# TensorE's tile loop takes in its first turn, and GpSimd holds the scatter of list two until that turn's matmuls are issued

## The reference: what is computed

```python
logits = jnp.einsum('btd,ed->bte', x, Wr)
probs = jax.nn.softmax(logits / TEMPERATURE, axis=-1)
topk_vals, topk_idx = jax.lax.top_k(probs, TOPK)            # TOPK = 2, E = 8
router_weights = topk_vals / topk_vals.sum(-1, keepdims=True)
gate = jnp.einsum('btk,btke->bte', router_weights, one_hot)
h = jax.nn.silu(jnp.einsum('btd,efd->btef', x, W1))         # DFF = 512
y = jnp.einsum('btef,edf->bted', h, W2)
out = jnp.einsum('bte,bted->btd', gate, y)
```

## Time and profile before

| | us |
|---|---|
| three runs, median (lowest, highest) | 1382.2 (1380.06, 1385.12) |
| the profiled execution | 1379.32 |
| its span, first to last instruction | 1377.4 |
| PE busy in the span | 962.4 (70%) |
| DVE busy | 857.2 (62%) |
| ACT busy | 729.5 (53%) |
| POOL busy | 445.7 (32%) |
| the chain that ended last: PE 38%, DVE 22%, "issue" 21%, ACT 13% | |
| mean granted clock of TensorE, as a share of 2.4 GHz | 0.858 |

### The profile page before, as it was taken

The page is one execution under the profiler, slowest core; times in us unless marked ns, Lnnn a source line. Parts: engine busy times, 40 slices in busy tenths (PEclk is TensorE's granted clock), DMA queues, the critical chain, the costliest instruction groups (busy, mean ns, idle before and its releaser), DMA issues.

```text
span 1377.4 us, 30644 instructions
## 1 busy us (share of the span) xinstructions
PE 962.4 (70%) x10082; PEld 815.0 (59%) x10083; DVE 857.2 (62%) x2598; ACT 729.5 (53%) x1364; POOL 445.7 (32%) x535
## 2 busy tenths in 40 slices
PE   4888888884999999999997402111698977676740
PEld 2777777773888888888886301000587866555530
DVE  3688888885788888888885730000454666566552
ACT  3666766653776767767763300000575765555531
POOL 3123333332010010010102357777002055654555
PEclk8989998887999999999997555555799999899985
DMA  6930000000001000000000002111233334443431
GB/s 193 290 87 15 15 15 15 15 9 18 13 11 21 10 11 17 10 19 10 0 1 1 1 38 71 51 59 52 55 93 86 92 95 106 99 107 99 101 87 53
DMA packets 157233, 73.72 MB, mean 54 GB/s; under 512 B 76034, under 2 KB 151042, under 8 KB 157188
## 3 DMA queue, kind: packets, MB, share of 16 engines
q1 hardware_dynamic: 148996, 56.34, 15.6%
q0 software_dynamic: 8192, 16.79, 4.2%
HBM read 22.76 MB, written 37.75 MB: 44 GB/s over the span
## 4 chain that ended last, share of the span: by engine, by line
PE 38%; DVE 22%; issue 21%; ACT 13%; another core or an unknown queue 2%; POOL 2%; DMA 1%; DVEq 1%; ACTq 0%; SPq 0%; POOLq 0%
PE bank L449 9%; PE bank L451 8%; PE bank L450 8%; PE bank L551 4%; DVE at L925 4%; DVE X L1002 3%; ACT XTa L746 3%; DVE mx L909 3%; ACT qzh L746 3%; PE bank L537 3%; PE bank L528 2%; DVE st L992 2%; ACT vz_self L755 1%; DVE z L937 1%
## 5 line engine op out<-in xcount | busy, mean ns | idle before, releaser
L424 POOL DMA_INDIRECT wst<-yd,pos x128 | 129.9, 1015 | 222.2 <-DVE z L1117 105.6
L449 PE MATMUL bank<-XTa,qzh 128*128 128x128 f16 x768 | 146.0, 226 | 37.7 <-ACT XTa L746 37.7
L925 DVE TENSOR_TENSOR at<-bank,rc 64x32 f32<-64x32 f32 (+1 forms) x768 | 153.5, 200 | 14.4
L831 ACT ACTIVATE pr<-bank 128x512 f32<-128x512 f32 x96 | 57.3, 597 | 192.4 <-remote 106.5
L760 ACT ACTIVATE pr<-bank 128x512 f32<-128x512 f32 x192 | 114.1, 594 | 79.5 <-PE bank L528 78.3
L909 DVE TENSOR_REDUCE mx<-bank 128x8 bf16<-128x512 f32 x192 | 132.9, 692 | 28.7 <-PE bank L451 23.1
L451 PE MATMUL bank<-XTa,qzl 128*128 128x128 f16 x768 | 146.5, 226 | 0.0
L450 PE MATMUL bank<-XTa,qzh 128*128 128x128 f16 x768 | 146.3, 226 | 0.0
L764 ACT ACTIVATE pt<-bank 128x512 f32<-128x512 f32 x192 | 113.3, 590 | 60.5 <-PE bank L537 60.1
L411 POOL DMA_INDIRECT xd<-XTa,pos x128 | 123.8, 968 | 65.3 <-issue 65.3
L1098 DVE TENSOR_TENSOR xtl<-xs,xth 128x512 f16<-128x512 f32 x96 | 66.4, 695 | 120.4 <-ACT xth L832 71.5
(11 more groups left out here) (202 smaller groups left out, 3084.5 us busy)
## 6 DMA issues: line engine op xcount, KB each, us to landing
yd<-at SPq DMA_DIRECT2D x96, 128.0 KB
xd<-blank SPq DMA_DIRECT2D x2, 3072.0 KB, 20.7
X<-x_dram SPq DMA_DIRECT2D x16, 256.0 KB, 2.8
wst<-w_dram SPq DMA_DIRECT2D x16, 256.0 KB, 2.7
xd<-blank SPq DMA_DIRECT2D x1, 4096.0 KB, 28.3
cin<-ctx_in_dram SPq DMA_DIRECT2D x16, 256.0 KB, 2.8
out_dram<-z SPq DMA_DIRECT2D x16, 256.0 KB
xd<-blank SPq DMA_DIRECT2D x1, 2048.0 KB, 21.5
```

The source lines that it names most:

```text
L424: nc.gpsimd.indirect_dma_start(out=yg[k][:, t, :], out_offset=None, in_=yd[chunk_of(n)], in_offset=bass.IndirectOffsetOnAxis(ap=pos[k][:, ...
L449: nc.tensor.matmul(out_, lh, rh, start=start, stop=False, **kw)
L831: nc.scalar.activation(s32[n % 4][:], bank[n % 4][:], ACT.Silu, scale=IWS)
L925: m = nc.vector.tensor_tensor(dst, src, r, ALU.mult)
```

## The change

Three edits. The straight copy of turn 0 goes, and the loop begins at turn 0; the word with the experts is moved into the loop's register ahead of it. Since the loop's first turns now also wait on `f_ev` (`down` waited from tile 2 on only), GpSimd adds 2 to `f_ev` beforehand by a memset of one column, and all waits on it are raised by 2. And GpSimd, before it scatters list two, waits until `f_h` is 10: the `up` matmuls of tiles 0 to 4, which stand 12 matmuls ahead of turn 0's end.

```diff
--- before.py
+++ after.py
@@ -272,7 +272,7 @@
                 sp.dma_start_transpose(xt[k], xd_v[c][bass.ds(n, 1)].rearrange("o r c -> (o r) c")).then_inc(ld_t[k], 16)
 
             def store(c, n, k):
-                wait_apart(sp, f_ev, n + CB[c] + 1, ld_w, 96)
+                wait_apart(sp, f_ev, n + CB[c] + 3, ld_w, 96)
                 sp.dma_start(yd_v[c][bass.ds(n, 1)].rearrange("o p r d -> p (o r) d"), yb[k]).then_inc(y_free[k], 16)
 
             def put(g):
@@ -387,6 +387,7 @@
             pool.wait_ge(sems["self"]["fin"], G)
             attention(CROSS, G)
             pool.wait_ge(sems["cross"]["fin"], G)
+            nc.gpsimd.memset(z2[:, 1, 0:1], 0.0).then_inc(f_ev, 2)
             nc.gpsimd.memset(z[:, 0, 0:1], 0.0).then_inc(z_free, 16)
             nc.gpsimd.memset(z2[:, 0, 0:1], 0.0).then_inc(f_fin, 1)
             for k in range(4):
@@ -404,6 +405,8 @@
             pool.wait_ge(r_pos, 2)
             pool.wait_ge(cleared, 16 * NC)
             for n, (t0, t1) in enumerate(SEGS):
+                if t0 == CHUNKS[1][0]:
+                    pool.wait_ge(f_h, 10)
                 if n >= 2:
                     pool.wait_ge(sent[n - 2], 32 * (SEGS[n - 2][1] - SEGS[n - 2][0]))
                 for t in range(t0, t1):
@@ -670,8 +673,8 @@
             def down(i, k, c, base):
                 n = 2 * (k % 2) + c
                 pe.wait_ge(f_sl, 2 * i + c + 1)
-                if c == 0 and not (isinstance(i, int) and i < 2):
-                    pe.wait_ge(f_ev, i - 1)
+                if c == 0:
+                    pe.wait_ge(f_ev, i + 1)
                 for h in range(2):
                     w = base + (2 * c + h) * 2 * P
                     for r in range(2):
@@ -705,10 +708,9 @@
             pe.wait_ge(ld_t[0], 16)
             for c in range(2):
                 up(0, c, offset(word, 0))
-            four(0, word, False)
-            with pe.Fori(1, NJ - 1) as j:
-                word = carried()
-                four(j, word, False)
+            pe.reg_mov(experts, word)
+            with pe.Fori(0, NJ - 1) as j:
+                four(j, carried(), False)
             four(NJ - 1, carried(), True)
```

## The result

| | before | the changed kernel |
|---|---|---|
| median, us (lowest, highest; 17 runs each) | 1382.11 (1375.66, 1390.83) | 1390.35 (1383.77, 1398.08) |
| the profiled execution's span, us | 1377.4 | 1392.9 |
| mean granted clock | 0.858 | 0.851 |

The ratio is 1.0064, with an interval of 1.0046 to 1.0082: slower by 8.2 us. The forecast was 1385.4 us and "no change", with a range of 1372 to 1402.

A forecast was written before the change was run, and what follows sets the result against it. TensorE was taken to be starved of instructions in turn 0 beside GpSimd's scatter DMAs. Moving this to turn 1 adds 3.2 us to the profiled 1379.3, 1382.5; the median lies 2.9 above, so 1385.4 us, range 1372 to 1402.

The forecast's parts named there:

- main step: TensorE beside GpSimd's indirect DMAs: code already in place is starved too, so starving moves to turn 1; within 6.9 us, 0.60.
- fast rival: Code in place is immune: turn 0 ends 120.7 us sooner, net -109.9, 1272.3 us; chance 0.15.
- The hold and the turn before it: GpSimd holds list two until 859.1, turn 0 ends at 860.1, and the scatter runs to 980.8, 18 us later.
- The tail: Starving of TensorE after the scatter's last DMA: 13.0 us scaled by stream length to 9.8; 13.0 would give +6.3.
- the 999: Sign in the profile after: turn 1 ending past 999 us, against 995 expected, would show the forecast wrong.
- The sum of the starved turn: Turn 1, starved from 863.4 to 990.6, ends at 995.5 against 992.24: +3.2 us on the path.
- slower rival: Turn 1 starves at once, without lead and with full tail: +11.5, 1393.7 us; slower cases together 0.20.
- the copy goes: 0 us: Turn 0's straight copy goes and the loop begins at turn 0: costs 0 us.
- the scatter spoils one turn: List two's and later scatter on GpSimd: whether it starves turn 0 or turn 1 matters little, +3.2 us.
- The stall of list two: Within immune code: list two lands at 922.0, tile 24 starts at 925.3 but is wanted at 914.5, +10.8 us.
- within 0.5%: Whole kernel: starving moves by one turn and the time stays within 6.9 us of before; chance 0.60.
- The slower case: Slower by over 6.9 us through no lead, full tail or a stall of turn 0's first pass; chance 0.20.

The follow-up runs named there:

- hold three: The changed kernel, but list two's scatter goes out unheld and lists three and four wait until f_h is 34; 1379.4 us against 1379.5 for the kernel before.
- hold short: The changed kernel with GpSimd's hold until f_h is 2 instead of 10; 1385.3 us against 1376.9 for the kernel before, ratio 1.0053.
- credit only: The kernel before with only 2 added to f_ev ahead and its waits raised by 2; 1378.6 us against 1377.7, ratio 0.9998.
- loop only: The changed kernel without GpSimd's hold; 1230.2 us against 1229.1 for the kernel before in the same job, ratio 1.0028.
- hold only: The kernel before with only the two lines of GpSimd's hold put in; 1238.4 us against 1229.1, ratio 1.0100.
- after again: The changed kernel, unchanged, timed in another job; 1242.6 us against 1227.9 for the kernel before, ratio 1.0127.
- before again: The kernel before, unchanged, run once more for its trace in another job; 1228.8 us against 1227.9.

## Why the prediction was right, and where its sum was short

**The main step was right**, for the condition that it was made in: starving needs no fresh code. Turn 1 ran in a body that had been executed, without a packet on q8 from 862 us on, and took 139 us; in "hold three" it happened in a body that had run four times. The row of turn 6 in the earlier trace rows that decided it was the right one to go by. The kernel before has a second one that I didn't use: its DMA view of 852 to 976 us, the whole starved stretch, has no q8 either, so even turn 0's own code wasn't starved by fetches on that queue. The fast rival (immune code in place, 1272 us) is refuted for the starving condition.

**That the condition was the same was luck.** The prediction takes for given that the changed kernel meets the starving of the profile before. It did. In a free job the same kernel took 1242.6 us, far outside the range of 1372 to 1402.

**The hold and the turn before it** came as worked out. This run's TensorE began 1.6 us later (846.95 for 845.34). GpSimd's 33rd DMA is at 861.05 (859.1 and 1.6 make 860.7), turn 0 ends at 860.85 (861.7 by the same shift), the first gap opens 3.7 to 4.3 us after the stream begins (4.3), and the last DMA is at 981.15 (981.2). Turn 1's end, 999.90, is past the 999 that was named as a sign of being wrong; without the 1.6 to 2.0 us by which this run lies later it is just under it. The gathers were far behind the scatter, as said (first at 1051.58, for 1046), and no new wait arose.

**The tail was mis-sized.** I scaled 13.0 us by the length of the stream to 9.8; it is 996.14 - 982.1 = 14.0, a little past the upper end that the text kept (13.0). What it goes with is the time that TensorE is starved beside the stream. Those that can be read: 13.0 us after 111 us (852 to 962.8, before), 14.0 after 117 (864.7 to 982.1, after), and 6.7 after 57 (953.4 to 1010.5, "hold three"); "hold short" has 13.2 after 115, "credit only" 13.7 after 110 and the first stream of "hold three" 6.3 after 49. That is 0.12 to 0.13 each time. The scatter that had passed ahead of TensorE's first matmul shouldn't have been counted in. For a short stretch the share doesn't hold: beside turn 6's gathers it was 1.6 us after 5.4.

**The sum of the starved turn, redone.** From the start of the stream to turn 1's end I had 136.4 us (859.1 to 995.5), and it took 138.9 (861.05 to 999.90). The tail gives +4.2. Against it stand 0.7 for the stream (121.05 us for 121.7) and 1.1 behind the recovery (3.76 us for 4.9): the slower rival's "no lead" was not met, 51 matmuls went through at full speed right behind the branch where I had 41, and 67 beside the stream where I had 60. So the stretch came 2.4 longer than worked out, and +3.2 becomes the +5.6 that the two profiles show. Two slips of the working (96 x 1.265 is 121.4, and the scaled tail 9.7) are worth 0.4 us.

**The step "the copy goes: 0 us" failed.** The loop that begins at turn 0 costs by itself: 1.0028 when free (loop only, 3.4 us, with an interval that just touches 0), and 3.5 us in turns 2 to 10 of "hold short" and of the changed kernel. I had counted the instructions of the body as unchanged. There are three more register additions in it and three waits fewer as instructions, and "credit only" shows that those are not the cause. Where the 3.5 us lie differs. In "hold short" every steady turn is 0.2 to 0.3 us longer, and turns 6 and 7, beside the gathers, 2.0 together. In the changed kernel the steady turns are at most 0.2 longer (11.36 to 11.64 us), turn 2 is 0.7 longer, and turns 6 and 7 are 1.4 and 1.0. In the sum: 5.6 for the hold and 3.5 for the loop are 9.1, against 8.2 measured. The third term of the profiled pair, 4.4 us behind turn 10, isn't in "hold short" (-0.1) and I take it for the spread of single executions, which is 14 us wide here.

**The time that a turn lost before** was not gained back since the stream is the same 96 DMAs, one every 1.27 us before and 1.264 after. That was the forecast's core, "the scatter spoils one turn", and it held. The stall of list two that stood in the fast rival (+10.8 us) was found where its condition was met, in the free jobs: turn 5 waits 11.0 us in "hold only" and 12.6 in "after again". I hadn't seen that the rival's world exists, with before at 1228 us, and that the change is slower there too (1.0127): the rival had put it 110 us faster, because it took the starving before for given.

**The chances**: "within 0.5%" had 0.60, and the measured 0.64% lies just past it, among the 0.20 for slower. With the starved turn alone the step would have been +5.6, still within the 6.9 us, and the loop's price takes it over. The slower case had no term for that, so its 0.20 was met by another road than the ones it named.

## What to carry to other kernels

A long stretch of "issue" beside GpSimd's indirect DMAs is not cured by moving the stream to another turn. Breaking it into pieces is, in good part: with four DMAs (5 us) to a piece, against some 50 matmuls (4 us) that TensorE still gets through, it took 61 us off, and left 4 to 8 us on each turn. If a hold is put on such a stream, count every list behind it against the turn that needs it; here one turn of hold was one turn of lateness. And before any of this is tuned, the kernel should be timed in several jobs: where the same program has two conditions, a schedule that wins in one can lose in the other.

## What the runs showed of the hardware

- The same program, on chips of the same number, took 1228.8 us in one job and 1379.5 (the kernel before beside "hold three") in another. The difference is in what TensorE gets beside indirect DMAs: 149 matmuls in a turn of 11.53 us, or 39 in 104.42. Of the 150.5 us between the spans of "before again" and of the kernel before, 121.6 lie between the first scatter DMA and turn 1's end, and nearly all the rest behind it, in turns with gathers. The stream's own pace hardly differs (1.27 and 1.29 us per DMA). With the one of the result, five jobs starved and three did not. The kernels of one job agreed, and what sets it stays open.
- Starving needs no packet on q8: there is none in the starved stretches of the kernel before (852 to 976 us), of the changed one (862 to 996) and of "hold three" (949 to 1018).
- In the starving condition TensorE's starving doesn't end with the stream. It ends after a further 0.12 to 0.13 of the time that it had lasted beside the stream, 14.0 us at the longest.
- A loop that takes in its first turn, with the body's instructions the same as in "credit only", has steady turns up to 0.3 us longer, and a turn 6 beside gathers of 20.2 to 20.3 us for 18.9 to 19.0. The cause wasn't found.
